# A layer norm's means and inverse roots written to device memory a word at a time, in the order in which they are read

## The reference

```python
xn = _layernorm(x, axis=-1)                    # (x - mean) / sqrt(var + 1e-5), for each token
x = x + _L0_attn_ref(xn, W_el, b_el, W_le, b_le) + _L0_ffn_ref(xn, w1, b1, w2, b2)
```

## Time and profile before

| | |
|---|---|
| median of three runs | 446.28 us (445.8 to 446.93) |
| the profiled execution: its own time | 446.24 us |
| the profiled execution: its span | 444.2 us |
| mean granted clock of TensorE over the span | 0.992 |
| busy: PE, DVE, ACT, POOL | 433.6, 298.0, 197.5, 80.0 us |
| rows_dram written, rows_sb read (each 15 times) | 4.0 KB in 1.4 us, 512.0 KB in 4.1 us from issue to landing, medians |

### The profile page before, as it was taken

The page is one execution under the profiler, slowest core; times in us unless marked ns, Lnnn a source line. Parts: engine busy times, 40 slices in busy tenths (PEclk is TensorE's granted clock), DMA queues, the critical chain, the costliest instruction groups (busy, mean ns, idle before and its releaser), DMA issues.

```text
span 444.2 us, 8446 instructions
## 1 busy us (share of the span) xinstructions
PE 433.6 (98%) x2856; PEld 391.5 (88%) x2856; DVE 298.0 (67%) x722; ACT 197.5 (44%) x332; POOL 80.0 (18%) x72
## 2 busy tenths in 40 slices
PE   7969999999999999999999999999999999999996
PEld 4858899899999999898998989989999999989996
DVE  5977586665767666576765667666575767667544
ACT  4742444444354344535443444444435434443431
POOL 1640211203013130301213012130401313030000
PEclk9997999999999999999999999999999999999999
DMA  8541302223130232303213230232313022020101
GB/s 236 169 168 48 120 2 90 101 71 118 50 110 29 71 118 71 118 15 99 76 71 118 71 116 2 82 108 71 118 45 106 38 71 71 24 71 5 44 24 49
DMA packets 17789, 35.38 MB, mean 80 GB/s; under 512 B 5331, under 2 KB 7533, under 8 KB 17773
## 3 DMA queue, kind: packets, MB, share of 16 engines
q1 hardware_dynamic: 17778, 35.24, 23.9%
HBM read 26.76 MB, written 8.45 MB: 79 GB/s over the span
## 4 chain that ended last, share of the span: by engine, by line
PE 91%; DMA 3%; POOL 2%; DVE 1%; ACT 1%; issue 1%; SPq 0%; DVEq 0%; POOLq 0%
PE p_o L786 40%; PE p_h L766 38%; PE p_c L800 11%; PE p_c L819 2%; DMA w_f<-L_ffn_w 1%; DMA rows_sb<-rows_dram 1%; PE p_g L810 1%; POOL xt_sb L333 1%; DMA rows_dram<-mv 1%; POOL w_lo L342 1%; PE p_c L872 0%; POOL mv L324 0%; DVE xt_sb L498 0%; DVE x_sb L602 0%; ACT w_hi L419 0%
## 5 line engine op out<-in xcount | busy, mean ns | idle before, releaser
L378 ACT ACTIVATE h<-p_h,b_sb 128x512 f32<-128x512 f32 x128 | 88.1, 689 | 213.0 <-PE p_h L766 213.0
L786 PE MATMUL p_o<-w_hi,h_hi 128*128 128x256 f32 x512 | 149.7, 292 | 4.1 <-DVE h_lo L508 4.1
L786 PE MATMUL p_o<-w_lo,h_hi 128*128 128x256 f32 x512 | 145.4, 284 | 0.0
L786 PE MATMUL p_o<-w_hi,h_lo 128*128 128x256 f32 x512 | 145.2, 284 | 0.0
L508 DVE TENSOR_TENSOR h_lo<-h,h_hi 128x512 fp32r<-128x512 f32 x128 | 94.6, 740 | 52.3 <-ACT h_hi L386 50.0
L786 PEld LDWEIGHTS p_o<-w_hi,h_hi 128*128 128x128 f32 x512 | 98.1, 192 | 7.1 <-DVE h_lo L508 4.7
L786 PEld LDWEIGHTS p_o<-w_lo,h_hi 128*128 128x128 f32 x512 | 98.3, 192 | 1.9
L786 PEld LDWEIGHTS p_o<-w_hi,h_lo 128*128 128x128 f32 x512 | 98.2, 192 | 0.0
L766 PE MATMUL p_h<-xT_hi,w_hi 128*128 128x512 f32 (+1 forms) x258 | 82.1, 399 | 0.6 <-ACT xT_hi L433 0.6
L386 ACT CAST h_hi<-h 128x512 fp32r<-128x512 f32 x128 | 79.5, 621 | 5.6
L766 PE MATMUL p_h<-xT_hi,w_lo 128*128 128x512 f32 (+1 forms) x258 | 79.9, 391 | 0.0
(11 more groups left out here) (95 smaller groups left out, 323.3 us busy)
## 6 DMA issues: line engine op xcount, KB each, us to landing
out<-x_sb SPq DMA_DIRECT2D x31, 256.0 KB, 2.3
x_sb<-L_attn_x SPq DMA_DIRECT2D x15, 512.0 KB, 5.3
xt_sb<-xt SPq DMA_DIRECT2D x15, 512.0 KB, 3.6
rows_sb<-rows_dram SPq DMA_DIRECT2D x15, 512.0 KB, 4.1
w_f<-L_ffn_w SPq DMA_DIRECT2D x3, 512.0 KB, 7.1
x_sb<-L_attn_x SPq DMA_DIRECT2D x2, 256.0 KB, 2.8
w_f<-L_ffn_w SPq DMA_DIRECT2D x2, 256.0 KB, 5.2
basis_sb<-basis SPq DMA_DIRECT2D x1, 256.0 KB, 4.9
```

The source lines that it names most:

```text
L378: nc.scalar.activation(h[m % 2][:], p_h[:, m % 2, :], ACT.Gelu, bias=b1_sb[:, m:m + 1]).then_inc(gelu_done, 1)
L786: last = mm(p_o[:, j, :], hp[r][:, tok], w[:, m, :], start=(m == 0 and n == 0 and j % 2 == 0), stop=(m == MB - 1 and n == 2), skip_group_c ...
```

## The change

rows_dram and rows_sb change their order: all means first, then all inverse roots, and within each by tile j and then by partition p. The write of mv, one DMA with 32 contiguous bytes from each partition, becomes two, one for the means and one for the roots, each of 128 x 4 single words, as neither side has two words of the transfer next to each other. Both count on the same semaphore, so that the wait ahead of the broadcast asks for twice as much. The broadcast still brings the same 4 KB to each of the 128 partitions. row_values then views 512 contiguous words, for POOL's line 333 and DVE's line 498.

```diff
--- before.py
+++ after.py
@@ -93,7 +93,7 @@
         xn = sb("xn", [P, CT, E], F32)
 
         xt_sb = [sb(f"xt_sb{i}", [P, KB, CTOK], F32) for i in range(2)]
-        rows_sb = [sb(f"rows_sb{i}", [P, P, CT, 2], F32) for i in range(2)]
+        rows_sb = [sb(f"rows_sb{i}", [P, 2, CTOK], F32) for i in range(2)]
         xT_hi = [sb(f"xT_hi{i}", [P, KB, CTOK], F32R) for i in range(2)]
         xT_lo = [sb(f"xT_lo{i}", [P, KB, CTOK], F32R) for i in range(2)]
         h = [sb(f"h{i}", [P, CTOK], F32) for i in range(2)]
@@ -198,7 +198,7 @@
 
         x_rows = x.rearrange("b s e -> (b s) e").rearrange("(p t) e -> p (t e)", p=P)
         out_rows = out.rearrange("b s e -> (b s) e").rearrange("(p t) e -> p (t e)", p=P)
-        rows_dram = nc.dram_tensor("rows_dram", (2, P, CT * 2), F32, kind="Internal").ap()
+        rows_dram = nc.dram_tensor("rows_dram", (2, 2, CT, P), F32, kind="Internal").ap()
         CW = CT * E
 
         def nth(c, par):
@@ -218,7 +218,7 @@
             return p_c[:, g, :].rearrange("p (k t) -> p k t", k=KB)
 
         def row_values(par, a):
-            return rows_sb[par][:, :, :, a].rearrange("p t j -> p j t")
+            return rows_sb[par][:, a, :].rearrange("p (j t) -> p j t", j=CT)
 
         block = ctx.enter_context(nc.Block())
 
@@ -260,12 +260,15 @@
                 sp.wait_ge(rstd_done, c + HEAD + 1)
                 if c > 2:
                     sp.wait_ge(rows_in[par], nth(c - 2, par))
-                sp.dma_start(rows_dram[par], mv[par][:, :, :].rearrange("p j a -> p (j a)")).then_inc(rows_out[par], 16)
-                sp.wait_ge(rows_out[par], nth(c, par))
+                with nc.allow_non_contiguous_dma(reason="4 KB a chunk, a word at a time"):
+                    for n in range(2):
+                        sp.dma_start(rows_dram[par, n].rearrange("j p -> p j"),
+                                     mv[par][:, :, n]).then_inc(rows_out[par], 16)
+                sp.wait_ge(rows_out[par], 2 * nth(c, par))
                 if c > 2:
                     sp.wait_ge(scaled, KB * (c - 2))
-                sp.dma_start(rows_sb[par][:, :, :, :].rearrange("p t j a -> p (t j a)"),
-                             rows_dram[par].rearrange("t a -> (t a)").partition_broadcast(P)).then_inc(rows_in[par], 16)
+                sp.dma_start(rows_sb[par][:, :, :].rearrange("p a t -> p (a t)"),
+                             rows_dram[par].rearrange("a j p -> (a j p)").partition_broadcast(P)).then_inc(rows_in[par], 16)
 
             def store_pair(c, q):
                 sp.wait_ge(pair_out, PRIMED + PAIRS * c + q + 1)
```

## The result

The kernel became a third slower: 593.87 us (median of four runs, 592.41 to 595.07) against 446.04 us (445.32 to 446.93, four runs beside them); the ratio is 1.331, its interval 1.327 to 1.335. The profiled execution took 594.4 us with a span of 592.2, 148.0 more than before. Lines of the new kernel lie 3 lower in the code: L333 is now L336, L498 is L501, L786 is L789, L810 is L813.

A forecast was written before the change was run, and what follows sets the result against it. TensorE was taken to bound the loop, so only the start before it could be shortened: 446.24 - 1.42 (earlier restart) - 0.4 (clock) = 444.4 us, range 442.4 to 446.9.

The forecast's parts named there:

- The reads: POOL's and DVE's reads of rows_sb, values side by side: 1.3 us from 1616 ns and 0.69 us from 1127 ns.
- The start: Before the loop: four operations end at 28.59 instead of 30.01, so TensorE restarts 1.42 us earlier.
- the clock: After TensorE's restart at the start: a shorter gap means less half-speed work, a gain taken as 0.4 us.
- The margin: In the loop: rows may come 1.47 + 0.20 = 1.67 us later before TensorE waits at the transpose.
- the four operations: POOL's two subtractions and DVE's two multiplications reading rows_sb: 3.98 us, against 5.98 at the start and 5.45 in the loop.
- This assumes that device memory takes words at the pace at which it takes 32 bytes, which no row shows: The write of the rows: assumption under which two word DMAs make the rows 0.58 us later.
- So I stay with the write's own row: The write of the rows: delay costed from the old write's 8.5 ns a packet, 0.58 us in all.
- b1: A load, the trace's only transfer by words, 6.4 us to landing against 1.4: upper bound of 5.0 us delay.
- the deciding point: In the loop: beyond 1.67 us of delay TensorE waits at the transpose in each of 14 chunks.
- Words are slow to be taken: Rival at the write: its tail grows eightfold to 2.6 us, rows 2.9 us late, about 464 us; chance 0.16.
- The order is not what makes the reads slow: Rival at the reads: four operations keep their times, 5.3 us lost in the loop, about 451.6 us; chance 0.06.
- The start gives too little: Rival at the start: rows 1.0 us later, gain 1.0, clock loss 0.5, about 445.7 us; chance 0.26.

The follow-up runs named there:

- read_only: The kernel before with its old write and broadcast, only the rows read side by side (values of other tokens): 444.5 us against 446.58, ratio 0.9952.
- late_2: read_only with the old write done three times, each awaited, so the rows come 2.9 us later: 463.45 us, ratio 1.037.
- probe: The kernel before with thirteen small transfers of varied piece size, spacing and memory appended, each awaited, list run twice; 512 words took 2.0 us to SBUF; total time means nothing.
- pitch: The kernel before with awaited small writes appended, mainly 128 words at growing distances: 7.24 us side by side, 1.42 at 16 bytes apart; total time means nothing.
- token_first: The kernel before with only chunk 1 of the turned x laid out by partition then tile, old write kept: 444.29 us, ratio 0.9954.
- token_order_2: token_order with the last hidden block's high and low parts put ahead of the second split: 443.97 us, ratio 0.9946.
- token_order: The kernel before with the turned x laid out by partition then tile in all chunks, old write kept: 451.2 us, ratio 1.012.

## Why the prediction was wrong

**What held.** TensorE bounds the loop, and a loss shows at the transpose, once in each of 14 chunks. The reads cost 1.26 and 0.68 us (forecast 1.3 and 0.69). The packets cost 7.7 ns each (8.5). The start gives a gain, 2.1 us when taken alone (read_only), where the forecast's terms without the words make 2.4. By the profiled execution the reads gave less of it than forecast and the clock more: from the broadcast's issue to TensorE's restart it is 11.83 us (21.61 to 33.44) in place of 13.38, 1.55 less and not 2.0, and 3.4 us at the lower level in place of 4.94 are worth half the difference, 0.77 and not 0.4. The margin is 1.72 to 1.87 us (1.67), and that it is so near is partly luck too: in late_2 the four operations give back 1.75 us (224.80 to 228.50, 3.70 us) and not 1.47, but POOL starts 4.75 us after the broadcast's issue and not 4.57.

**The step that failed** is "This assumes that device memory takes words at the pace at which it takes 32 bytes, which no row shows", and behind it "So I stay with the write's own row": 0.58 us of delay, where the runs show 9.5. The row I scaled was the packets' time on the engines, and that did scale as I said. But SP goes on only when the write has been acknowledged, and this part, from the last packet on, went from 0.33 us to 9.1. I had bounded the delay at 5.0 us by b1, a transfer by words; it is a load, whose words are written to SBUF, and probe shows that SBUF takes 512 words in 2.0 us. So the bound came from a row that did not bear on the cost at all. And the stated range did not even reach that bound: its high end stops at the deciding point of 1.67 us of delay.

**The rival that came true** is "Words are slow to be taken", to which I gave 0.16. Its place and its deciding point were right, its size was not: I let the tail grow with the number of pieces, eightfold to 2.6 us. The tail goes by how densely the pieces lie (pitch), and came out 27 times as long. A price was missing as well: I counted a wait in the loop as idle time alone. After a wait of 7.86 us TensorE works at 1.2 GHz for 6.11 us, 2.84 us a chunk on top. The waiting itself follows the way the prediction reckoned: in the chunk shown POOL starts 15.99 us after the first word's issue in place of 6.01, the four operations take 1.82 us less and 0.20 was slack, so 9.98 - 2.02 = 7.96 us of waiting (7.86 measured).

**The argument that misled me.** The old pieces too are short, and landed in 1.4 us, so I took the trace to speak against a great price for short pieces. That holds for 32 bytes and says nothing of four. The Trainium skill (DMA: Bandwidth & Descriptors, Specifications) has the engines read, change and write back below 512 bytes; its direction was right for this change, but its threshold is not what these runs show: 32-byte pieces and words 16 bytes apart are both far below it and take 1.41 and 1.42 us, and what takes longer lies more densely. The Trainium skill (DMA: Bandwidth & Descriptors, Anatomy of one DMA), on transfers that GpSimd issues, puts most of a transfer's fixed time into the receipt from the memory written, the heaviest being device memory. The 9.1 us without a packet, here on SP's queue, agree with where it puts the time, though not with its some 2 us.

**The rival on the order of the reads** ("The order is not what makes the reads slow") is out: read_only changes the order alone and is faster. (Its 451.6 us also leaves out the 0.58 us that the start would lose.) **The start** gave enough: of "The start gives too little" nothing is left once the words are gone. How much of the start's gain is the clock's was not tried apart; after the restart the profiled executions run at the lower level for about 2.9 us (token_first), 3.4 (read_only) and 3.5 (token_order_2), against 4.94 before, and in token_order not at all.

## What to carry to other kernels

Before a transfer is split into smaller pieces, ask what memory it ends in and how densely the pieces will lie there: packets on the engines are visible in the profile, the acknowledgement behind them only as a wait of the issuer with a share of 0.00. Where an order is wanted for the reader's sake, change the layout that the host hands over or the view of an operation that has slack, and keep the pieces written at the 32 bytes that cost 1.4 us here. And price a wait of TensorE's with the lower clock behind it, not with the idle time alone: it stood behind the wait of 7.86 us, while behind the one of 1.03 us in late_2 (at 230.99) the clock stayed at 1.00.

## What was not expected of the hardware

128 words side by side (512 bytes in all) take 7.24 us to be acknowledged, five times as long as 4 KB in 32-byte pieces (1.41). With 16 bytes from one word to the next that is gone. Words that nobody waits for can still hold up others: in 5 of 15 chunks the broadcast of 512 KB came late beside them, at the worst after 10.8 us, where without them none took more than 4.5. And an operation of 512 columns that reads fp32 values 16 bytes apart takes 1.12 us on ACT and 1.09 on DVE, against 0.61 and 0.69 side by side, while POOL at 8 bytes apart pays next to nothing (1.31 against 1.30 us).
